# Summing pairs of chunks on GpSimd before TensorE's column strips, in the ternary FFN of a two-layer kernel

## The reference

```
h = einsum('btd,hd->bth', x, absmean(W_fc))      # 8 batches, 512 tokens, 256 -> 1024
h = gelu(h, approximate=False)
h = layernorm(h, ln_w, ln_b)                     # over the 1024
y = einsum('bth,dh->btd', h, absmean(W_proj))    # 1024 -> 256
x = layernorm(x + y)                             # over the 256
```

## Time and profile before

| | |
|---|---|
| median of 3 runs | 1071.32 us (1071.27 to 1071.67) |
| the profiled execution, its own time | 1073.13 us |
| span of its trace, first to last instruction | 1071.4 us |
| mean granted TensorE clock | 0.929 of full speed |
| first and last start of `up`'s matmuls in the ternary FFN | 335.4 and 500.6 us |
| last VectorE operation of the ternary FFN ends | 520.1 us |

### The profile page before, as it was taken

How to read it: one execution, slowest core, us unless ns; L and a number is a source line. 1 busy time by engine, 2 the same in 40 slices (tenths; PEclk the granted TensorE clock), 3 DMA queues, 4 the chain that set the end, 5 groups by cost and what they waited for, 6 DMA issues and landing times. The chain is left out here.

```text
span 1071.4 us, 22452 instructions
## 1 busy us (share of the span) xinstructions
PE 866.7 (81%) x8200; PEld 683.6 (64%) x8200; DVE 695.9 (65%) x1512; ACT 480.4 (45%) x1112; POOL 230.6 (22%) x316
## 2 busy tenths in 40 slices
PE   3787888788866999998498978998878956999950
PEld 3676666666655777776243447777566745999950
DVE  5346656665664577777588962577878796465528
ACT  1343443344335777775296433455344222444320
POOL 0212121212121022212200000002233113656323
PEclk9899999999996999999699989999988957999995
DMA  7100000000000000000047745546121310556438
GB/s 237 26 12 21 10 20 10 20 10 20 0 1 1 1 1 1 1 2 1 5 119 159 182 108 109 117 106 202 50 79 56 102 50 28 156 153 184 119 66 267
DMA packets 74613, 75.25 MB, mean 70 GB/s; under 512 B 26032, under 2 KB 68144, under 8 KB 73392
## 3 DMA queue, kind: packets, MB, share of 16 engines
q1 hardware_dynamic: 70576, 69.08, 22.4%
q0 software_dynamic: 3968, 5.25, 3.0%
HBM read 46.51 MB, written 27.79 MB: 69 GB/s over the span
## 5 line engine op out<-in xcount | busy, mean ns | idle before, releaser
L594 DVE TENSOR_TENSOR r_prob<-r_pS,const 128x512 f32<-128x512 f32 x128 | 79.5, 684 | 41.8 <-PE r_pS L464 41.8
L1089 DVE SCALAR_TENSOR_TENSOR f_gl<-f_g,lnw,f_gh 128x512 fp32r<-128x512 f32 x64 | 47.3, 747 | 40.8 <-ACT f_gh L1027 38.5
L1325 PE MATMUL q_pE<-q_xT,att_res 128*128 128x512 f32 x128 | 60.9, 631 | 6.2 <-ACT q_xT L1264 6.2
L968 PE MATMUL f_pY<-wpjT,f_gh 128*128 128x256 f32 x256 | 65.2, 289 | 0.0
L969 PE MATMUL f_pY<-wpjT,f_gl 128*128 128x256 f32 x256 | 62.8, 279 | 0.0
L968 PEld LDWEIGHTS f_pY<-wpjT,f_gh 128*128 128x128 f32 x256 | 48.1, 188 | 15.2 <-issue 13.4
L585 DVE COPY r_kT<-r_pKK 128x256 f32<-128x256 f32 x32 | 13.6, 424 | 64.9 <-PE r_pKK L449 64.9
L1021 ACT ACTIVATE f_g<-f_pH 128x512 f32<-128x512 f32 x64 | 38.1, 595 | 39.0 <-PE f_pH L957 38.3
L2254 POOL DMA_INDIRECT sum_dram<-e_yo,y_id x24 | 39.5, 1646 | 70.1 <-ACT e_yo L2343 60.9
L957 PE MATMUL f_pH<-f_xh,wfcT 128*128 128x512 f32 x128 | 53.0, 414 | 1.4 <-DVE f_xl L1083 1.4
L372 ACT ACTIVATE r_rT<-r_pXR 128x128 f32<-128x128 f32 x64 | 17.8, 278 | 78.3 <-PE r_pXR L504 77.5
(11 more groups left out here) (305 smaller groups left out, 2527.2 us busy)
## 6 DMA issues: line engine op xcount, KB each, us to landing
kv_dram<-att_res SPq DMA_DIRECT2D x16, 512.0 KB, 4.3
t_ring<-kv_dram SPq DMA_DIRECT2D x128, 64.0 KB, 2.3
wi<-L_ffn_wi SPq DMA_DIRECT2D x8, 1024.0 KB
wo<-L_ffn_wo SPq DMA_DIRECT2D x8, 1024.0 KB
xin<-L_attn_x SPq DMA_DIRECT2D x32, 128.0 KB, 2.0
q_dram<-att_res SPq DMA_DIRECT2D x8, 512.0 KB, 2.9
t_q<-q_dram SPq DMA_DIRECT2D x64, 64.0 KB, 3.3
x_dram<-x_res SPq DMA_DIRECT2D x8, 512.0 KB, 3.0
```

What stands on the lines that cost most here:

```text
L594: dve.tensor_tensor(prob[t % 2][:, r, :, :], pS[r][:, :, :], dec[:, r, :, :], ALU.mult)\
L968: pe.matmul(out, gh[c % 4][:, cols], net.wpjT[:, c, :], start=(c == 0 and t % 2 == 0), stop=False, skip_group_check=True)
L1089: dve.scalar_tensor_tensor(out=gl[c % 4][:, :], in0=g[c][:, :], scalar=net.lnw[:, c:c + 1], in1=gh[c % 4][:, :], op0=ALU.mult, op1=ALU.sub ...
L1325: mm = pe.matmul(out[:, :], net.wqkvT[:, k, n * P:(n + 1) * P], xT[p][:, k, :], start=(k == 0), stop=(k == KD - 1))
```

## The change

GpSimd gets a new piece of work, `pair(b, p)`: it adds the Gelu values of chunks 2p and 2p + 1 into a new tile `g2[p]`, and their squares into `gg[2p]`, each an addition of 128x512 values with all operands in SBUF. `sum_strips` then reads four tiles a call (two of sums, two of squares) where it read eight, so that four matmuls, one in each strip, stand for eight. It waits for `paired` where it waited for `squared`. On TensorE, `sum_strips` moves from c = 6 to c = 7 and from c = 1 to c = 2 of the next batch, `gather_sums` from c = 3 to 4; on ScalarE `keep_sums` from c = 2 to 3; on VectorE the block of `norm` and `base` from c = 1 to 2 and `moments` from c = 3 to 4, and at the very end `moments` comes behind `norm` and `base`. `gelu(b, c)` waits for `paired` of the batch before where it waited for `summed`, and `square` of an even chunk now waits for `summed`. GpSimd's queue for a batch is: pair 3 of the batch before, `outer` of the batch before that, pair 0, `inner` of the batch before, pairs 1 and 2.

```diff
--- before.py
+++ after.py
@@ -918,7 +918,7 @@
     xh, xl = ([ph.sb(f"{n}{i}", [P, KD, SEQ], F32R) for i in two] for n in ("xh", "xl"))
     g, gg = ([ph.sb(f"{n}{i}", [P, SEQ]) for i in range(NH)] for n in ("g", "gg"))
     gh, gl = ([ph.sb(f"{n}{i}", [P, SEQ], F32R) for i in four] for n in ("gh", "gl"))
-    strips = ph.sb("strips", [P, SEQ])
+    strips, g2 = ph.sb("strips", [P, SEQ]), [ph.sb(f"g2{i}", [P, SEQ]) for i in four]
     y, xb = ph.sb("y", [P, TPB, DIM]), ph.sb("xb", [P, TPB, DIM])
     both, var, rs, shift = ph.sb("both", [P, TPB, 2]), ph.sb("var", [P, TPB]), ph.sb("rs", [P, TPB]), ph.sb("shift", [P, TPB])
     yst, ymv, yrs = ph.sb("yst", [P, TPB, 6]), ph.sb("ymv", [P, TPB, 2]), ph.sb("yrs", [P, TPB])
@@ -929,6 +929,7 @@
     pB = pS[:, 0:TPB * 2].rearrange("p (t s) -> p t s", s=2)
     turned, xh_ready, xl_ready = (ph.sig(n) for n in ("turned", "xh_ready", "xl_ready"))
     up_made, gelued, high, split, squared = ph.sig("up_made"), ph.sig("gelued", 2), ph.sig("high"), ph.sig("split", NH), ph.sig("squared")
+    paired = ph.sig("paired", NH // 2)
     down_made, y_taken = ph.sig("down_made", 4), ph.sig("y_taken", 2 * TPB)
     summed, sums_kept, sums_made, sums_taken = ph.sig("summed", 2), ph.sig("sums_kept"), ph.sig("sums_made"), ph.sig("sums_taken")
     var_ready, rs_ready, rows_ready, yrs_ready = (ph.sig(n) for n in ("var_ready", "rs_ready", "rows_ready", "yrs_ready"))
@@ -971,13 +972,13 @@
 
         def sum_strips(b, q):
 
-            pe.wait_ge(squared.sem, squared.after(NH * b + 4 * q + 4))
+            pe.wait_ge(paired.sem, paired.after(NH // 2 * b + 2 * q + 2))
             if q == 0:
                 pe.wait_ge(sums_taken.sem, sums_taken.after(b))
-            for c in (4 * q, 4 * q + 2):
-                for s in range(4):
-                    part = (g, gg)[s % 2][c + s // 2]
-                    mm = pe.matmul(pS[32 * s:32 * s + 32, :], net.table["ones"][:, 0:32], part[:, :], start=(c == 0), stop=(c == NH - 2))
+            for s in range(4):
+                c = 2 * q + s // 2
+                part = gg[2 * c] if s % 2 else g2[c]
+                mm = pe.matmul(pS[32 * s:32 * s + 32, :], net.table["ones"][:, 0:32], part[:, :], start=(q == 0), stop=(q == 1))
             mm.then_inc(summed.sem, 1)
 
         def gather_sums(b):
@@ -993,11 +994,11 @@
             for c in range(NH):
                 if b < BATCH:
                     up(b, c)
-                if b and c == 1:
+                if b and c == 2:
                     sum_strips(b - 1, 1)
-                if b and c == 3:
+                if b and c == 4:
                     gather_sums(b - 1)
-                if b < BATCH and c == 6:
+                if b < BATCH and c == 7:
                     sum_strips(b, 0)
                 if b < BATCH and c >= 2:
                     down(b, c - 2)
@@ -1016,7 +1017,7 @@
         def gelu(b, c):
             n = NH * b + c
             act.wait_ge(up_made.sem, up_made.after(n + 1))
-            act.wait_ge(summed.sem, summed.after(2 * b + c // 4 - 1))
+            act.wait_ge(paired.sem, paired.after(NH // 2 * (b - 1) + c // 2 + 1))
             act.wait_ge(split.sem, split.after(n + 1 - NH))
             nc.scalar.activation(g[c][:, :], pH[c % 2][:, :], ACT.Gelu).then_inc(gelued.sem, 1)
 
@@ -1028,6 +1029,8 @@
 
         def square(b, c):
 
+            if c % 2 == 0:
+                act.wait_ge(summed.sem, summed.after(2 * b + c // 4 - 1))
             nc.scalar.activation(gg[c][:, :], g[c][:, :], ACT.Square).then_inc(squared.sem, 1)
 
         def keep_sums(b):
@@ -1045,7 +1048,7 @@
                     square(b, c - 1)
                 if c == NH - 1:
                     square(b, c)
-                if b and c == 2:
+                if b and c == 3:
                     keep_sums(b - 1)
                 if b + 1 < BATCH and c in (3, 6):
                     take(b + 1, (c - 3) // 3)
@@ -1070,9 +1073,28 @@
             pool.wait_ge(steps.sem, steps.done(1))
             rstd_of(pool, steps, mean_square, mean_square, RMS_EPS, net).then_inc(q_rs_ready.sem, 1)
 
+        def pair(b, p):
+
+            pool.wait_ge(squared.sem, squared.after(NH * b + 2 * p + 2))
+            if b:
+                pool.wait_ge(summed.sem, summed.after(2 * (b - 1) + p // 2 + 1))
+            pool.tensor_tensor(g2[p][:, :], g[2 * p][:, :], g[2 * p + 1][:, :], ALU.add)
+            pool.tensor_tensor(gg[2 * p][:, :], gg[2 * p][:, :], gg[2 * p + 1][:, :], ALU.add).then_inc(paired.sem, 1)
+
         for b in range(BATCH):
-            inner(b)
-            outer(b)
+            if b:
+                pair(b - 1, 3)
+            if b > 1:
+                outer(b - 2)
+            pair(b, 0)
+            if b:
+                inner(b - 1)
+            pair(b, 1)
+            pair(b, 2)
+        pair(BATCH - 1, 3)
+        outer(BATCH - 2)
+        inner(BATCH - 1)
+        outer(BATCH - 1)
 
     @block.vector
     def _(dve):
@@ -1178,9 +1200,9 @@
                     rows(b - 1, c - 5)
                 if b and c == NH - 1:
                     rows(b - 1, TPB - 1)
-        moments(BATCH - 1)
         norm(BATCH - 2)
         base(BATCH - 1)
+        moments(BATCH - 1)
         shifts(BATCH - 1)
         last_rows(BATCH - 1)
         norm(BATCH - 1)
```

## The result

| | before | after |
|---|---|---|
| median of all runs | 1071.49 us (1071.27 to 1075.12, 4 runs) | 1092.67 us (1088.98 to 1093.66, 4 runs) |
| ratio | | 1.0183, 95% interval 1.0150 to 1.0216 |
| profiled execution, its own time | 1073.13 us | 1093.66 us |
| first matmul of `up` in the ternary FFN | 335.39 us | 335.66 us |
| first TensorE work of the next stage | 522.6 us | 542.5 us |

The changed kernel is slower by 1.8%, 19.6 us by the ratio, which is one of means; the medians differ by 21.2 us. The stage of the change lasts 19.6 us longer; the spans differ by 20.6, so nearly all of it is there.

The account below looks back on a forecast made before the run. TensorE sets the pace in the ternary FFN (busy 21.12 of 21.25 us a batch). Batches +5.1 to +15.3, first batch -1.2, tail +2.1 to +4.5 give +6.0 to +18.6, middle +12.3: median 1084 us, range 1064 to 1097.

Parts of the forecast that it names:

- What bounds the kernel, and what leaves TensorE: Ternary FFN: TensorE sets the pace, 21.12 of 21.25 us a batch; two rounds fewer per `sum_strips` call save 13.8 us.
- the walk: Step-by-step timing of one ternary FFN batch from the end of `up` of chunk 0; 19.53 us without delays.
- The collision: GpSimd additions (10.2 us a batch) and VectorE's two-SBUF-input operations (9.2) exclude each other: 19.4 of 19.5 us.
- the lock seldom lands: Rival, chance 0.20: additions seldom hold VectorE off; batch 19.53 plus 0.4 us, 1061 us, faster.
- break-even: Rival, chance 0.18: VectorE mostly keeps its turn, TensorE waits only for `paired`; batches 21.0 to 21.5 us, 1070 to 1076.
- Which operations: FFN operations of VectorE with two SBUF inputs: `gl` 0.75, `xb` 0.48, `base` 1.23 us; 9.2 us a batch.
- order one: GpSimd wins the race at 14.4 us in the batch; next `up` 1.8 us late, `gl` 0 another 2.1 to 2.4; batch 23.8.
- worse than both orders: Rival, chance 0.12: late pairs delay `inner`, `shifts` and rows, pair 0 hits `base` and `gl` 3, 4; 25 us batches, 1092 to 1100.
- The two orders: Who wins GpSimd against VectorE at pair 1: GpSimd first, batch 23.8 us; VectorE's `shift` and `xb` first, 22.1 us.
- The clock: TensorE's granted clock in the FFN should stay full, so no loss; otherwise part of the loss is the clock's.
- The tail: Behind the last FFN batch: 25.4 us from `up` 5 to the last norm becomes 27.5 to 29.9, +2.1 to +4.5.
- The sum: Batches, first batch and tail together +6.0 to +18.6 us, middle +12.3: 1085.4 us profiled, 1084 for the median.

Follow-up runs that it names:

- short additions: The changed kernel with each GpSimd addition cut to 4 of 512 columns, sums left incomplete: 1063.04 us, ratio 0.9916.
- pair 1 first: The changed kernel with pair 1 ahead of `inner` in GpSimd's queue: 1084.53 us, ratio 1.0108.
- places alone: The kernel before with the moved calls and queue orders of the change, but no additions: 1075.03 us, ratio 1.0024.
- additions alone: The changed kernel with TensorE summing all eight chunks and waiting for `squared`, the additions going into tiles nobody reads: 1090.36 us, ratio 1.0164.
- accumulating DMAs: The changed kernel with each GpSimd addition replaced by an in-place accumulating DMA in SBUF, issued by GpSimd: 1093.61 us, ratio 1.0194.

## Why the prediction was right, point by point

**What bounds the kernel, and what leaves TensorE.** Right. Two rounds less a call give 19.53 us by the walk and 19.96 in the run with short additions; between them is the wait for `keep_sums` that the moved places bring (0.58 us a batch), which the prediction had put at nothing.

**The price of an addition.** Right: 1.28 us from the line through the earlier trace rows, 1.26 us the shortest measured.

**The collision.** Right, and shown from three sides: additions without length are harmless, GpSimd work of nearly the same length that reads nothing is harmless, additions that nobody on TensorE waits for cost nearly as much as the change. The rival that the lock seldom lands is out; so is break-even, in which VectorE keeps its turn: the two sides alternate, and both lose. The 64 additions are busy for 97.5 us, 1.52 us each where 1.28 was their price. One piece of the prediction's evidence was read too far, though: of the two `gl` beside the root in the earlier trace rows the second took its usual 0.74 us and followed the first without a gap, so those rows show that GpSimd waits, and not that it gets in ahead of VectorE. That it does is shown by the changed kernel alone.

**Which operations.** The list of operations that an addition on GpSimd holds off was short by two: `shift`, 4 columns wide, waited to 1.25 us at the median of eight (the walk lets it wait in order one alone), and `norm`, with one SBUF input besides its column values, had a maximum of 1.38 us where its median was 0.41 (the walk lets it wait nowhere). That happened to two of 32, both in the longest batch:

```profile
408.99 1.33 POOL L1081 TENSOR_TENSOR f_g<-f_g 128x512 f32<-128x512 f32 x1
409.09 3.32 DVE L1180 TENSOR_SCALAR x_res<-f_y,f_ymv,f_yrs 128x256 f32<-128x256 f32 x4
```

Here `norm` came late, 14.8 us behind the first `sum_strips` of the batch where the other five have 11.8 to 13.6, and pair 0 met it. In the other five pair 0 met `gl` of chunk 3 (1.42 to 1.65 us), and TensorE did not wait for it. Both are of the kind that the rival worse than both orders describes, with `norm` where it named `base`. The median of 1092.67 us lies just above the forecast's own range (1077 to 1092) and at the lower end of that rival's, so the two share the result.

**The two orders.** The sum took their middle, since the race was to fall differently from batch to batch. It fell the same way: `shift` and the `xb` behind it were held off in seven of eight batches, order one; `gl` of chunk 5 just before them was held off too in five of the seven (1.76 to 1.85 us), which the order did not have. TensorE's gaps are where that order put them, the first and largest before `up` of the next batch (1.8 us expected, 1.6 to 2.9 measured). The second, for `gl` of chunk 0, was given as 2.1 to 2.4 us and was at most 0.6. By its times the walk had pair 3 beside rows 2 and 3. In the trace the six additions followed each other more closely (391.25 to 399.82 in the worst batch, 8.6 us where the walk has 10.4), pair 3 met `gl` of chunk 6 and row 1, and in every batch it was over before row 2, here by 2 us:

```profile
401.86 0.48 DVE L1141 SCALAR_TENSOR_TENSOR f_xb<-u_both,f_shift,f_xb 128x256 f32<-128x256 f32 x1
```

The batch of order one came to 23.8 us, 24.1 measured, with another make-up: the walk has 19.5 us of work and 3.9 to 4.2 of waits, the trace 20.8 of work and 3.3 of waits (2.1 for `xl`, 0.6 for `strips`, 0.4 for pairs, 0.2 for `gl`). That the two are so close is in part luck.

**The clock.** This is the term that was missing. The prediction set the clock's part at zero and said that it would show otherwise. Behind waits of 1.8 to 2.9 us TensorE ran at the lower level in four of six batches: from 398.5 to 405.3, 449.7 to 453.1, 473.6 to 477.0 and 497.5 to 500.9. By the windows above (1 less the granted clock, by the length) that is 3.4 + 1.7 + 1.7 + 1.7 = 8.5 us. TensorE's busy time rose by about 7.2 of them, counted against the two batches at full clock, which have 19.76 and 19.77 us. (These have 0.4 us more than the 19.38 of the short additions, without any loss of clock.)

Not all of it lay on the path. The first and the fifth batch began with the same wait for `xl` (1.77 and 1.76 us), the first at full clock, the fifth with a fall: 22.98 and 23.85 us. TensorE was busy 1.50 us longer and the batch only 0.87, since a wait of 0.55 us for `gl` was gone. With pair 1 first it is the same, 22.57 us at full clock and 23.47 to 23.51 with a fall, behind waits of 1.7. By such comparisons the four falls made their own batches longer by about 5 us together (an estimate: 2.3, 0.9, 0.9 and 0.9). On the other side, behind the two batches at full clock the next one began with a wait of 2.84 or 2.87 us, behind three with a fall with 1.63 to 1.78. So the clock's part of the 19.6 us is under 8.5, and how large it is stays open.

**The tail.** From the last `up` (its end at 514.96 us, the call of `sum_strips` at 515.83 less its wait of 0.87) to the end of the last norm (540.0) are 25.1 us, where the earlier trace rows have 19.1, so 6.0 more. (The prediction took 500.85 as the end of the last `up` before; 500.61 and 0.40 make 501.01.) Order one had put this at 6.5 (11.5 + 14.2 against 5.5 + 13.7).

```profile
525.25 0.18 DVE L1151 BATCH_NORM_AGGREGATE f_ymv<-f_yst 128x2 f32<-128x6 f32 x1
...
538.64 1.38 DVE L1180 TENSOR_SCALAR x_res<-f_y,f_ymv,f_yrs 128x256 f32<-128x256 f32 x4 [1.52 <-POOL f_yrs L712]
```

From the last row of batch 6 to the last norm are 14.6 us, 13.7 before and 14.2 in the prediction: the later `moments` costs 0.9 us where 0.5 was said. In all, 1.8 of the 6.0 us come from the places, as the runs with places alone and with short additions show.

**The sum.** +12.7 us forecast on the medians; +21.2 measured so, +19.6 by the ratio. The step that was mis-sized is the batch: 22.1 to 23.8 with the middle taken, 24.1 measured. Order one alone would have given +18.6. The direction and the mechanism were right; that 1092.67 us still lies within the stated 1064 to 1097 it owes to the room left above both orders.

## What to carry to other kernels

Work that reads SBUF and is moved to GpSimd was not free here, since VectorE's operations with two SBUF inputs left it no room: add both up over one period, and look at the bunch in which they come, not at either engine's share. Where an engine waits on the path, the price is not only the wait: TensorE can come back at half clock (here it was busy some 7 us longer for it, part of it on the path, beside a loss of 19.6). To part such causes, keep the length and drop the reads (memsets), and keep the work and drop its consumer.

## What the runs showed of the hardware

- A GpSimd instruction that only writes does not hold VectorE's two-input operations off: 64 memsets of 1.17 us, and 64 `gl` with a maximum of 0.754 us. A GpSimd addition that reads two tiles, begun together with `gl` at 396.88, held it off until it ended at 398.14; `gl` ended 0.55 us later, at 398.69.
- The width of the VectorE operation that is held off made no difference here: one of 4 columns waited as long (1.25 us for 0.16, seven times of eight) as one of 512 (1.85 for 0.75).
- The granted clock fell to its lower level behind some of TensorE's waits and not behind others of the same length. In the changed kernel and in the run with pair 1 first there are eight waits of 1.63 to 1.78 us in the batches; five were followed by a fall, three were not (those that ended at 375.3 and 424.4 us in the one and at 420.9 in the other). The fall can come when TensorE is busy again: the wait from 470.6 to 472.3 was followed by one at 473.6, and full clock came back at 477.0. All eight waits of 2.15 to 2.87 us in the batches of the changed kernel and of the accumulating DMAs were followed by a fall; six of 1.22 us with additions alone were not. What decides between waits of the same length was not tried.
- An accumulating DMA from SBUF to SBUF, 256 KB, landed 3.5 us (of Gelu values) and 4.4 us (of squares) behind its issue at the median, with the two issued together, and issuing it delayed no `gl` (maximum 0.772 us).
